# Sparsemax thresholds of flagged pairs: eight more candidates in place of the sum over the row

## The reference, cut to what matters

```python
def sparsemax(z):
    n = z.shape[-1]
    z_sorted = jnp.flip(jnp.sort(z, axis=-1), axis=-1)
    cssv = jnp.cumsum(z_sorted, axis=-1)
    r = jnp.arange(1, n + 1, dtype=z.dtype)
    support = 1.0 + r * z_sorted > cssv
    k = jnp.sum(support, axis=-1, keepdims=True)
    tau = (jnp.take_along_axis(cssv, k - 1, axis=-1) - 1.0) / k.astype(z.dtype)
    return jnp.maximum(z - tau, 0.0)
...
sim = jnp.einsum('bhid,bhjd->bhij', q, k) * SCALE
attn = sparsemax(sim)
out = jnp.einsum('bhij,bhjd->bhid', attn, v)
```

## Time and profile before

| what | value |
|---|---|
| median of three runs | 872.06 us |
| profiled execution, its own time | 873.6 us |
| its span | 871.7 us |
| PE busy | 675.0 us (77%) |
| DVE busy | 598.2 us (69%) |
| ACT busy | 456.4 us (52%) |
| POOL busy | 201.8 us (23%) |
| mean granted clock of PE | 0.878 of full speed |

### The profile page before, as it was taken

One profiled execution on the slowest core, in us unless ns is written; L12 is line 12 of the kernel. 1 busy time (PEld: TensorE's weight loads), 2 busy tenths in 40 slices (PEclk: granted clock), 3 DMA queues, 4 the chain that ended last, 5 costly groups with the idle time before them and its releaser, 6 DMA issues. The chain is left out here.

```text
span 871.7 us, 12946 instructions
## 1 busy us (share of the span) xinstructions
PE 675.0 (77%) x4060; PEld 447.2 (51%) x4060; DVE 598.2 (69%) x2170; ACT 456.4 (52%) x664; POOL 201.8 (23%) x212
## 2 busy tenths in 40 slices
PE   4687869867999999999999998673323788887380
PEld 2344355455576575575765756452212666664360
DVE  2777797878987979988779689836888455541020
ACT  2967656537867776778677787642001232332020
POOL 1000000001001000010010100001006688888875
PEclk9889988969999999999999998885555899999595
DMA  5200000000000000000000000006001144354333
GB/s 163 84 1 0 2 1 2 0 2 14 2 2 14 2 2 14 2 14 2 2 14 1 2 13 2 14 1 163 0 0 40 46 68 70 76 90 65 39 33 27
DMA packets 34717, 23.67 MB, mean 27 GB/s; under 512 B 8232, under 2 KB 31226, under 8 KB 34628
## 3 DMA queue, kind: packets, MB, share of 16 engines
q0 software_dynamic: 11264, 8.40, 7.1%
q1 hardware_dynamic: 23152, 14.21, 5.8%
q10 hardware_dynamic: 212, 0.08, 0.1%
HBM read 14.29 MB, written 8.39 MB: 26 GB/s over the span
## 5 line engine op out<-in xcount | busy, mean ns | idle before, releaser
L549 ACT ACTIVATE front<-ps 128x1024 f32<-128x1024 f32 x128 | 127.7, 1027 | 37.4 <-PE ps L796 12.8
L646 ACT ACTIVATE front<-front,minus_tau 128x256 f32<-128x256 f32 x256 | 108.6, 497 | 37.6 <-DVE minus_tau L1191 36.5
L549 ACT ACTIVATE back<-ps 128x1024 f32<-128x1024 f32 x72 | 73.7, 1024 | 94.4 <-PE ps L926 82.0
L517 POOL DMA_INDIRECT out_dram<-back x64 | 100.5, 1570 | 23.8 <-issue 22.6
L455 POOL CROSS_LANE_REDUCE more_all<-more 128x1 int32<-128x1 f32 x32 | 11.5, 358 | 398.4 <-DVEq L1116 265.3
L829 PE MATMUL ps<-ident,front 128*128 128x128 f32 x512 | 75.0, 295 | 30.0 <-ACTq L648 21.6
L829 PEld LDWEIGHTS ps<-ident,front 128*128 128x128 f32 x512 | 63.3, 151 | 52.6 <-ACTq L648 31.7
L549 ACT ACTIVATE back<-ps,back 128x1024 f32<-128x1024 f32 x32 | 35.6, 1113 | 103.1 <-PE ps L940 103.1
L504 POOL DMA_INDIRECT back<-rows,back x64 | 64.2, 1003 | 69.6 <-issue 66.9
L954 PE MATMUL ps<-back 128*128 128x128 f32 x512 | 67.6, 300 | 6.0 <-ACT back L549 4.5
L845 PE MATMUL ps<-back,front 128*64 128x256 f32 x512 | 70.8, 408 | 1.2 <-ACT back L549 1.2
(11 more groups left out here) (190 smaller groups left out, 1082.8 us busy)
## 6 DMA issues: line engine op xcount, KB each, us to landing
back<-in_L_ffn_W_dram SPq DMA_DIRECT2D x16, 256.0 KB, 3.4
front<-in_x_dram SPq DMA_DIRECT2D x4, 750.0 KB, 4.5
rows<-xn SPq DMA_DIRECT2D x8, 256.0 KB, 2.2
out_dram<-h SPq DMA_DIRECT2D x1, 2048.0 KB, 7.8
back<-rows,back POOLq DMA_INDIRECT x64, 2.5
out_dram<-back POOLq DMA_INDIRECT x64, 3.3
wqkv<-in_L_attn_W_qkv_dram SPq DMA_DIRECT2D x1, 768.0 KB, 5.7
back<-in_L_ffn_b_dram SPq DMA_DIRECT2D x8, 64.0 KB, 3.7
```

The lines of the kernel that those rows point to most:

```text
L517: g.indirect_dma_start(orow[:, :], bass.IndirectOffsetOnAxis(ap=add_at[p][:, s:s + 1], axis=0), y[p][:, s, :], None, compute_op=ALU.add)\
L549: a.activation(dst, ps[s][:, 0:cols], func, **kw).then_inc(sems[f"free{s}"], 1)
L646: a.activation(prob[n % 2][:, r, :], sc[n][:, r, :], ACT.Relu, bias=minus_tau[:, n // 2, n % 2 * 4 + r:n % 2 * 4 + r + 1])
```

## The change: what it does

When a pair is flagged, DVE no longer sums the rows. It runs the new `third_eight`: it strikes the second eight out of `sc2` in place, keeps their sum from `csum` (place 15 less place 7) in `r_sum`, finds the next eight, scans again over places 0 to 15 of `top` (now the first and the third eight), forms the eight candidates for n = 17 to 24, takes their largest, and raises `tau` to it where it is higher. Then it counts the rows whose 24th largest score lies above the new `tau` and brings that count down to one word by the same eight small steps, now a function `decide`. Only if that word is set, `rest_of_refinement` runs: `surplus` once and then up to 26 steps of `newton` in one loop, where there were two steps written out and a loop of 24. POOL fills a new constant `inv24` with eight small memsets at the start.

```diff
--- before.py
+++ after.py
@@ -264,6 +264,7 @@
         more_all = sb("more_all", [P, 4, 1], i32)
         seg16 = sb("seg16", [P, 8, 16])
         inv16 = sb("inv16", [P, 8, 16])
+        inv24 = sb("inv24", [P, 8])
         r_sum = sb("r_sum", [P, 8])
         r_cnt = sb("r_cnt", [P, 8])
         go_w = sb("go_w", [P, 32])
@@ -440,6 +441,8 @@
             g.memset(seg16[:, :, 0:1], 0.0)
             for n in range(16):
                 g.memset(inv16[:, :, n:n + 1], 1.0 / (n + 1))
+            for n in range(8):
+                g.memset(inv24[:, n:n + 1], 1.0 / (n + 17))
             g.drain()
             g.engine_nop().then_inc(sems["const"], 1)
 
@@ -1115,6 +1118,47 @@
                                        accum_out=more[:, d, :])
                 v.drain().then_inc(sems["more_ok"], 1)
 
+            def decide():
+                v.drain()
+                v.transpose(go_t[:, :], go_w[:, :])
+                v.drain()
+                v.tensor_reduce(go_s[:, 0:1], go_t[:, :], AX.X, ALU.max)
+                v.drain()
+                for k in range(4):
+                    v.tensor_copy(go_4[0:1, k:k + 1], go_s[32 * k:32 * k + 1, 0:1])
+                v.drain()
+                v.tensor_reduce(go_s[0:1, 0:1], go_4[0:1, :], AX.X, ALU.max)
+                v.drain()
+
+            def third_eight(d):
+                t = top[d % 2]
+                for r in range(8):
+                    v.match_replace(sc2[:, r, :], t[:, r, 8:16], sc2[:, r, :], LOWEST)
+                v.tensor_tensor(r_sum[:, :], csum[:, :, 15], csum[:, :, 7], ALU.subtract)
+                v.drain()
+                for r in range(8):
+                    v.max(t[:, r, 8:16], sc2[:, r, :])
+                v.drain()
+                v.tensor_tensor_scan(csum[:, :, :].rearrange("p r n -> p (r n)"),
+                                     seg16[:, :, :].rearrange("p r n -> p (r n)"),
+                                     t[:, :, :].rearrange("p r n -> p (r n)"), 0.0, ALU.mult, ALU.add)
+                v.drain()
+                v.scalar_tensor_tensor(cand[:, :, 8:16], csum[:, :, 8:16], -1.0,
+                                       r_sum[:, :].unsqueeze(2).to_broadcast([P, 8, 8]), ALU.add, ALU.add)
+                v.drain()
+                v.tensor_tensor(cand[:, :, 8:16], cand[:, :, 8:16],
+                                inv24[:, :].unsqueeze(1).to_broadcast([P, 8, 8]), ALU.mult)
+                v.drain()
+                v.tensor_reduce(r_cnt[:, :], cand[:, :, 8:16], AX.X, ALU.max)
+                v.drain()
+                v.tensor_tensor(tau[:, d, :], tau[:, d, :], r_cnt[:, :], ALU.max)
+                v.drain()
+                v.scalar_tensor_tensor(above[:, :], t[:, :, 15], 1.0, tau[:, d, :], ALU.mult, ALU.is_gt,
+                                       accum_out=go_w[:, 0:1])
+                decide()
+                v.tensor_scalar(go[0:1, :], go_s[0:1, 0:1], 0.5, None, ALU.is_gt)
+                v.drain()
+
             def surplus(d):
 
                 for r in range(8):
@@ -1123,16 +1167,7 @@
                                            ALU.subtract, ALU.max, accum_out=r_sum[:, r:r + 1])
                 v.drain()
                 v.tensor_reduce(go_w[:, 0:1], r_sum[:, :], AX.X, ALU.max)
-                v.drain()
-                v.transpose(go_t[:, :], go_w[:, :])
-                v.drain()
-                v.tensor_reduce(go_s[:, 0:1], go_t[:, :], AX.X, ALU.max)
-                v.drain()
-                for k in range(4):
-                    v.tensor_copy(go_4[0:1, k:k + 1], go_s[32 * k:32 * k + 1, 0:1])
-                v.drain()
-                v.tensor_reduce(go_s[0:1, 0:1], go_4[0:1, :], AX.X, ALU.max)
-                v.drain()
+                decide()
                 v.tensor_scalar(go[0:1, :], go_s[0:1, 0:1], -1.0, 3e-6, ALU.add, ALU.is_gt)
                 v.drain()
 
@@ -1158,15 +1193,13 @@
 
             def rest_of_refinement(d):
 
-                newton(d)
+                surplus(d)
                 with v.If(go_on()):
-                    newton(d)
-                    with v.If(go_on()):
-                        with v.Fori(0, 24):
-                            with v.If(go_on()):
-                                newton(d)
-                            v.drain()
+                    with v.Fori(0, 26):
+                        with v.If(go_on()):
+                            newton(d)
                         v.drain()
+                    v.drain()
                 v.drain()
 
             settled = Tally(None)
@@ -1182,7 +1215,7 @@
                     ahead.append(v.mark_branch_hint_location())
                 v.br_ne(wide, 0, f"refine{n}", f"settled{n}").branch_hint(hint)
                 with nc.body(f"refine{n}", valid_engines=[mybir.EngineType.DVE]):
-                    surplus(d)
+                    third_eight(d)
                     v.br_ne(v.value_load(go[0:1, 0:1], min_val=0, max_val=1), 0, f"rest{n}", f"settled{n}")
                 with nc.body(f"rest{n}", valid_engines=[mybir.EngineType.DVE]):
                     rest_of_refinement(d)
```

More of the change, by code:

```diff
@@ L1116, in laced_thresholds @@
                 v.drain().then_inc(sems["more_ok"], 1)
[L1118 to L1123, removed]
-                v.drain()
-                v.tensor_reduce(go_w[:, 0:1], r_sum[:, :], AX.X, ALU.max)
+            def decide():
                 v.drain()
@@ L1135, in surplus @@
                 v.drain()
+            def third_eight(d):
[26 more added lines that the diff above has]
+                v.drain()
+            def surplus(d):
+                for r in range(8):
+                    v.scalar_tensor_tensor(sc2[:, r, :], sc[2 * d + r // 4][:, r % 4, :], tau[:, d, r:r + 1],
+                                           zero[:, :].to_broadcast([P, SEQ]),
+                                           ALU.subtract, ALU.max, accum_out=r_sum[:, r:r + 1])
+                v.drain()
+                v.tensor_reduce(go_w[:, 0:1], r_sum[:, :], AX.X, ALU.max)
+                decide()
                 v.tensor_scalar(go[0:1, :], go_s[0:1, 0:1], -1.0, 3e-6, ALU.add, ALU.is_gt)
```

## The result

The changed kernel takes **882.01 us** (881.01 to 883.6, 6 runs); the kernel before took 872.33 us beside it (868.32 to 874.09, 6 runs). The ratio is 1.0121, with an interval of 1.0097 to 1.0145: slower by 9.7 us. The forecast was 886 us, that is 14.1 us slower, with a range of 877 to 893.

A forecast was written before the change was run, and what follows sets the result against it. No engine bounds the whole span; longer DVE checks behind pairs C, D and E land on PE's path. Net delays run from 2.8 us earlier through 3.4 and 7.9 to 14.1 later: 873.6 + 14.1 = 887.7, against the median 886 us; range 877 to 893.

The forecast's parts named there:

- The check: DVE's new check at each flagged pair: 9.7 us, 4.5 more than the old; its three small steps 230 ns each.
- rival 4: 24 candidates do not suffice at pair A, so `surplus` still runs behind: 892.5 us; chance 0.02.
- Pair A: Flagged pair without its Newton step now: `minus_tau` 8.7 us earlier, PE's idle 10.01 us shrink to about 1.
- Pair B: Next flagged pair on DVE: check 4.5 us later, DVE net 4.2 earlier, PE waits about 12, L782 2.8 earlier.
- Pair C: Flagged pair before the first norm: + 4.5, PE waits 5.5 us, clock + 1.7, net 3.4 later; stall kept.
- rival 2: Both DVE stalls vanish without a new one and PE's clock holds: 878 us; chance 0.15.
- Pair D: Flagged pair before the first norm: + 4.5 on DVE, PE's slack 1.57 us, all kept, net 7.9 later; stall kept.
- Pair E: Last of the five flagged pairs: + 4.5, PE waits some 8 us, clock + 1.7, net 14.1 later.
- To the end: Behind pair E: PE sets the pace, DVE has room at every norm, so 14.1 us stay to the end.
- Rival 1: Rounds' room of 7.8 us hides three checks, PE's wait behind C stays near 1 us: 868 us; chance 0.08.
- Rival 5: DVE's passes in place run faster or POOL's and ACT's timing shifts favourably: under 863 us; chance 0.02.
- the upper of 891: Rival that the longer check runs into two more stalls on DVE: 886 + 5 = 891 us; chance 0.2.

The follow-up runs named there:

- e_only_a: Against the kernel before: the new check at pair A alone, the old check at the other flagged pairs; ratio 0.9973, stretch 463.6 us.
- e_only_c: Against the kernel before: the new check at pair C alone, the old check at the other flagged pairs; ratio 1.0101, stretch 478.2 us.
- e_long_rest: Changed kernel with its never-run rest of the refinement written out as long as before; ratio 1.0144 against the kernel before, stretch 484.6 us.
- s_before_64: Kernel before with 64 drains more at DVE's very start, nothing else changed; ratio 0.9979 against the kernel before, stretch 469.1 us.
- e_old_check_short: Kernel before with its old check, only the rest of the refinement shortened from three copies of newton to two; ratio 1.0001, stretch 468.3 us.
- s_before_128: Kernel before with 128 drains more at DVE's very start, nothing else changed; ratio 1.0 against the kernel before, stretch 468.8 us.
- s_after_64: Changed kernel with 64 drains more at DVE's start; ratio 1.0208 against the kernel before, 897.28 us against 878.22, stretch 491.8 us.
- e_max_twice: Changed kernel with the eight MAX8 of the third eight done twice, 2.8 us more per check; ratio 1.0331 against the kernel before, stretch 496.8 us.
- e_only_e: Against the kernel before: the new check at pair E alone, the old check at the other flagged pairs; ratio 1.0042, stretch 473.1 us.

## Why the prediction was right, and where it was not

- **The check: right.** 9.7 us forecast, 9.6 measured at C; the small steps are 0.23 us as taken. Forty replacements at L1136, no sum over 256 scores and none of Newton's counts: rival 4 did not happen.
- **Pair A: right in mechanism.** 7.9 us earlier, not 8.7, since a stall of 0.8 us stands in its check. PE's wait is 2.08, not 1. e_only_a gives the term without that stall: 8.7.
- **Pair B: right.** Forecast 4.2 us earlier on DVE and 2.8 on PE's way; 3.3 and 3.2 measured, with a wait of PE of 10.5 for 12. That the 2.8 came so near is in part luck: the clock was 0.80 over the 8 us behind B, so 1.6 us were lost and not the 3.1 taken for so long a wait, and this met the 0.9 us that DVE gained less.
- **Pair C: this step failed.** Forecast 3.4 us later, measured 1.1 earlier, a miss of 4.5. I kept its stall of 2.51 us, and so put PE's wait at 5.5 us and added 1.7 for the clock. The stall vanished, the wait was 3.08 and the clock 1.00. That is rival 2 at one pair. e_only_c and e_long_rest show the same pair with the stall: waits of 5.40 and 5.63 us, and the loss as forecast. s_before_64 shows that it goes when nothing but the place of the code is changed.
- **Pair D: right in size, wrong in its reading.** It added 4.4 us on DVE (4.5 forecast), PE's wait was 2.78 ("near 3"). But what I called D's stall of 2.44 us is none. Places change in e_old_check_short, s_before_64 and s_before_128, and it stays (2.38, 2.38, 2.45). In the changed kernel and in five more traces it is named a wait for ACT, in after 2.23 us. From the start of the norm to this addition it is 327.09 - 323.53 = 3.56 us before and 328.82 - 325.48 = 3.34 after. It reads as the way through PE and ACT and back, and behind a PE clock of 0.52 in s_after_64 the idle time before the addition grew to 4.36. No run took that way apart.
- **Pair E: right, its clock too small.** 4.2 us between D and E on DVE for 4.5. PE waits 6.29 us for 8: the 4.4 us behind D, at 0.61, had already cost it 1.7 us, for which the forecast had nothing and which DVE, the bound there, did not feel. Behind E 8 us at 0.67 lose 2.6 us, 0.9 more than the 1.7 taken.
- **To the end: nearly right.** 10.1 us stay from there. A later pair adds 1.3 us by stalls of 0.63 and 0.95 us that the kernel before had not. The start gives 1.4 and the experts 1.0 back; the prediction had nothing for either.

The terms of the stretch: 14.1 - 4.5 (C) + 0.9 (clock behind E) + 1.3 (late stalls) - 0.4 (left over from the other places) = 11.4 us. Rival 1 is out: PE's wait behind C grew to three times, and all that was added to a check in e_max_twice came out at the end. Rival 5 is out by the time itself.

I took the count of stalls as plus or minus two. With 64 drains the same program lost 13.6 us of stretch, through five, because those at B, C and D brought clock with them. My lower rival of 878 us and the upper of 891 priced this too narrowly.

What stays open: why the first `minus_tau` comes at 97.6 to 100.0 us in eight traces and at 103.6 to 105.2 in six. It is not the place of DVE's code: e_only_c and e_only_e have the same program of DVE up to there, ran on the same chip, and start at 98.2 and 105.0. It may change from one execution to the next; the six times of the kernel before fall into two groups too, 868.3 to 868.9 and 872.1 to 874.1 us. One trace for each kernel can't tell. The stalls are steadier: the one in A's Newton step is 2.57, 2.59 and 2.76 us in before, e_only_c and e_only_e, whose code on DVE is the same up to it. Open too is what the stalls are: they follow the place of the code, and the Trainium skill, Runtime: NRT & Kernel Launch, section Instruction fetch mechanics, has a rule that would fit those behind a branch, a wait for a page of code that is not yet there. That the place decides agrees with it; but several stalls here stand in straight code, in the middle of the eight strikes or between two copies, and the trace names no releaser, so no run here proves it.

## What to carry to other kernels

Before replacing a check by a dearer one that saves a rare repair, multiply: four pairs paid 4.5 us each for one that gained 8.7. Put it only where the repair happens, if that is known. And where a long unrolled program has stalls that nothing releases, shift the code by some 64 instructions and measure again, both the kernel before the change and the one after it, or an effect of 1% is not told from a change of place. Here the same change measured 1.0121 without the shift and 1.0241 with both kernels shifted; the new check at A alone measured 0.9973, with 1 inside its interval, and 0.9946.

## What the runs showed of the hardware

- Stalls on DVE that no engine releases are 2.25 to 2.76 us each for most, some 0.8 to 1.8. They stood behind branches, in the middle of straight code and at pairs with no flag. 64 instructions of shift moved, removed or added them; 128 left the two largest of the kernel before in place (2.57 and 2.45 us).
- A mean clock below 1.00 followed waits of PE of 2.78 us (0.61), 1.94 and 1.99 us (both 0.79), and did not follow waits of 3.08 and 1.98 (both 1.00). The wait alone does not tell it. Behind each of the waits from 5.17 to 14.49 us in the rounds it was lost.
- A step of 128x64 on DVE takes 226 ns on the mean, between 170 for 128x8 and 293 for 128x128.
